# One-hots of source places kept in DRAM by the first edge pass and loaded by the other three, in a four-layer graph network on Trainium2

## The reference, cut to what matters

```python
# L0: two rounds of
agg = segment_sum(x[src], dst, num_segments=n_nodes)
h = (1.0 + eps) * x + agg
h = relu(h @ wa + ba) @ wb + bb
# L3: two rounds of
for r in range(8):
    mask = (edge_type == r)
    s = segment_sum(x[src] * mask[:, None], dst, num_segments=n)
    cnt = segment_sum(mask, dst, num_segments=n)
    out = out + (s / clip(cnt, 1.0)[:, None]) @ W[r]
```

## Time and profile before

| | |
|---|---|
| median of 3 runs | 8339.17 us (8332.13 to 8340.34) |
| profiled execution, first to last instruction | 8339.0 us |
| busy: TensorE matmul, weight load | 77%, 63% |
| busy: VectorE, ScalarE, GpSimd | 59%, 34%, 62% |
| first and second pass | about 1366 to 1760 us and 1805 to 2191 us of the span |
| third and fourth pass | about 7014 to 7592 us and 7650 to 8304 us of the span |
| mean of a group, by starts of its gather: first, second, third, fourth | 2.15, 2.16, 1.60, 1.81 us |

### The profile page before, as it was taken

How to read it: one execution, slowest core, us unless ns; L and a number is a source line. 1 busy time by engine, 2 the same in 40 slices (tenths; PEclk the granted TensorE clock), 3 DMA queues, 4 the chain that set the end, 5 groups by cost and what they waited for, 6 DMA issues and landing times. The chain is left out here.

```text
span 8339.0 us, 233485 instructions
## 1 busy us (share of the span) xinstructions
PE 6397.8 (77%) x55084; PEld 5290.0 (63%) x55143; DVE 4889.1 (59%) x13551; ACT 2862.7 (34%) x8539; POOL 5197.0 (62%) x7407
## 2 busy tenths in 40 slices
PE   2222215767699998999899989999976666888998
PEld 1111113555477776888688868887475556887998
DVE  6333346867556654666466646665432225998998
ACT  3222202545333333333333333333233332222554
POOL 3777755756477776777577757776577774222554
PEclk7555556555599999999999999999555556999999
DMA  5000013434388886888688868887300001332232
GB/s 163 3 3 3 3 38 113 120 96 121 94 223 216 216 204 179 222 222 222 164 222 222 222 163 226 222 222 184 100 6 7 7 7 35 82 82 56 72 73 59
DMA packets 1322718, 1020.15 MB, mean 122 GB/s; under 512 B 479756, under 2 KB 1223586, under 8 KB 1321696
## 3 DMA queue, kind: packets, MB, share of 16 engines
q1 hardware_dynamic: 938010, 667.14, 29.1%
q0 software_dynamic: 134272, 178.98, 11.0%
q10 hardware_dynamic: 250308, 172.51, 7.1%
HBM read 951.88 MB, written 73.77 MB: 123 GB/s over the span
## 5 line engine op out<-in xcount | busy, mean ns | idle before, releaser
L1607 POOL DMA_INDIRECT qg<-q_tab,qidx x2520 | 2388.6, 948 | 928.8 <-issue 692.8
L1762 DVE COPY ps<-b 128x384 f32<-128x384 f32 x1120 | 628.1, 561 | 1355.7 <-ACT h L1727 1348.1
L1156 PE MATMUL ps<-rhs_i,ohi 128*128 128x128 f32 (+2 forms) x8640 | 1215.5, 266 | 210.3 <-issue 198.3
L1156 PEld LDWEIGHTS ps<-rhs_i,ohi 128*128 128x128 f32 (+1 forms) x8640 | 999.1, 162 | 343.2 <-issue 281.9
L1122 POOL COPY near<-x 128x48 bf16 x2160 | 676.0, 351 | 775.9 <-PE ps L1145 433.2
L1676 PE MATMUL ps<-ohm,h 128*128 128x128 f32 x6720 | 1032.1, 290 | 61.3 <-DVE ps L1762 30.7
L1307 POOL DMA_INDIRECT got_m<-y_tab,idx_m x832 | 832.9, 1001 | 344.6 <-issue 246.3
L1720 ACT ACTIVATE h<-ps,b 128x384 f32<-128x384 f32 x1120 | 651.2, 581 | 1049.3 <-PE ps L1658 964.1
L1676 PEld LDWEIGHTS ps<-ohm,h 128*128 128x128 f32 x6720 | 838.5, 191 | 252.0 <-issue 237.0
L406 POOL DMA_INDIRECT list_by_src<-ring,rpos x808 | 783.0, 969 | 333.0 <-issue 254.2
L1781 DVE TENSOR_SCALAR ohm<-iota_row,loc_p,w_p 128x128 f32<-128x128 f32 x3360 | 963.1, 354 | 0.1
(11 more groups left out here) (441 smaller groups left out, 8601.8 us busy)
## 6 DMA issues: line engine op xcount, KB each, us to landing
pb<-p_tab ACTq DMA_DIRECT2D x1680, 96.0 KB
pb<-p_tab SPq DMA_DIRECT2D x1680, 96.0 KB
places<-place_by_turn SPq DMA_DIRECT2D x560, 192.0 KB
places_i<-place_by_meeting SPq DMA_DIRECT2D x360, 256.0 KB, 3.4
places_i<-place_by_meeting SPq DMA_DIRECT2D x720, 128.0 KB, 3.1
qb<-q_tab SPq DMA_DIRECT2D x840, 64.0 KB
qg<-q_tab,qidx POOLq DMA_INDIRECT x2520
nears<-near_by_turn SPq DMA_DIRECT2D x560, 64.0 KB
```

What stands on the lines that cost most here:

```text
L1156: m = pe.matmul(ps[:, bass.ds(to[j], width)], ohi[:, h, j, :], rhs[:, h, j, 0:width], start=False, stop=True, skip_group_check=True)
L1607: pool.indirect_dma_start(qg[:, h, j, :], None, q_tab, IndirectOffsetOnAxis(ap=qidx[:, h, j:j + 1], axis=0)).then_inc(m_got[h], 16)
```

## The change

In the first pass, SyncE writes each group's `oht` to a new table in DRAM, `oht_tab` (180 blocks of 256 KB, 47 MB), after it has been built, and VectorE waits for that write (`i_kept`) before it builds into the same slot again. In the other three passes VectorE builds no `oht`; SyncE loads it from the table into the same ring, once the gather of group n-4 is done (`i_got`). TensorE's gather waits for that load (`i_pl`) instead of for `i_oh`, and its sums wait for `i_oh` too, since `ohi` is still built.

```diff
+        oht_tab = dram("place_onehots", [NIN // 8, P, 8 * P], BF16)
...
+        i_kept = [sem(f"i_kept{h}") for h in range(U)]
...
-                places = sb(f"places_i{turn}", [P, U, M * P], BF16, st)
+                places = sb(f"places_i{turn}", [P, U, M * P], BF16, st) if first else None
...
+                        def keep(k, h):
+                            sp.dma_start(oht_tab[bass.ds(k * U + h, 1), :, :].rearrange("a p e -> (a p) e"), oht[:, h, :]).then_inc(i_kept[h], 16)
+
                         def fetch(k, h):
                             n = k * U + h
+                            if first:
+                                if here(k, h, U):
+                                    sp.wait_ge(i_oh, g0 + n - U + 1)
+                                    keep(k - 1, h)
+                                sp.dma_start(places[:, h, :], place_i[0:1, bass.ds(n * M * P, M * P)].to_broadcast([P, M * P])).then_inc(i_pl[h], 16)
+                                return
                             if here(k, h, U):
-                                sp.wait_ge(i_oh, g0 + n - U + 1)
-                            sp.dma_start(places[:, h, :], place_i[0:1, bass.ds(n * M * P, M * P)].to_broadcast([P, M * P])).then_inc(i_pl[h], 16)
+                                sp.wait_ge(i_got, g0 + n - U + 1)
+                            rows = (oht_tab[bass.ds(k * (U // 2) + h // 2, 1), :, (h % 2) * M * P:(h % 2 + 1) * M * P] if masked else
+                                    oht_tab[bass.ds(n, 1), :, :])
+                            sp.dma_start(oht[:, h, :], rows.rearrange("a p e -> (a p) e")).then_inc(i_pl[h], 16)
                         turns(sp, fetch, rounds)
+                        if first:
+                            for h in range(U):
+                                sp.wait_ge(i_oh, g0 + ng - U + h + 1)
+                                keep(rounds - 1, h)
+                            for h in range(U):
+                                sp.wait_ge(i_kept[h], 16 * rounds)
...
-                            pe.wait_ge(i_oh, g0 + n + 1)
+                            if first:
+                                pe.wait_ge(i_oh, g0 + n + 1)
+                            else:
+                                pe.wait_ge(i_pl[h], 16 * (k0 + k + 1))
...
                             pe.wait_ge(i_rhs, g0 + n + 1)
+                            if not first:
+                                pe.wait_ge(i_oh, g0 + n + 1)
...
-                            dve.wait_ge(i_pl[h], 16 * (k0 + k + 1))
-                            dve.tensor_scalar(oht[:, h, :], places[:, h, :], iota_p[:, 0:1], None, ALU.is_equal)
+                            if first:
+                                if here(k, h, U):
+                                    dve.wait_ge(i_kept[h], 16 * k)
+                                dve.wait_ge(i_pl[h], 16 * (k0 + k + 1))
+                                dve.tensor_scalar(oht[:, h, :], places[:, h, :], iota_p[:, 0:1], None, ALU.is_equal)
```

More of the change, by code:

```diff
@@ L1065, in edge_pass @@
             masked = mode in ("third", "fourth")
-            fourth, third = mode == "fourth", mode == "third"
+            fourth, third, first = mode == "fourth", mode == "third", mode == "first"
             M = 4 if masked else 8
```

## The result

| | before | after |
|---|---|---|
| median | 8339.76 us (8332.13 to 8341.28, 4 runs) | 8407.93 us (8406.37 to 8409.80, 4 runs) |
| span of the profiled execution | 8339.0 us | 8406.7 us |
| ratio after to before | | 1.0083 [1.0068, 1.0097] |

The kernel got slower by 68 us, where +27 was forecast. The direction was right, the size too small, and the measured time lies 13 us above the range, which ended at 8395.

A forecast was written before the change was run, and what follows sets the result against it. TensorE's sequencer was taken to bound the second and most of the first pass, VectorE the fourth, both engines nearly even in the third. On 8339.0 us, 23 + 18 - 11 - 3 + 0 = +27 gave 8366 us; range 8290 to 8395.

The forecast's parts named there:

- Second pass: TensorE's sequencer sets the pace; 180 added waits and 45 register instructions cost +23 us, bounds 0 and +26.
- I take 0.105 us per group for the wait: Sums' added wait on TensorE's sequencer: 0.105 us per group, from 0.32 us for three such instructions; its own duration is 51 ns.
- Third pass: VectorE and TensorE close to even; +0.05 us for each of 360 groups, +18 us, bounds -20 and +38.
- I take half of that: Third pass: half of the +38 us that would come if all four intervals of a round grew by 0.105 us.
- the 1.40 chain: Third pass: gather, mask, gather in 1.40 us; does not run over the sums, so has room for most of the wait.
- Fourth pass: VectorE sets the pace before; afterwards 1.78 us per group against 1.81, so -11 us, bounds -40 and 0.
- The list (1.70, 1.70, 1.78, 1.94): Fourth pass: forecast us from gather to gather by position in the round, longer after and into its top; mean 1.78.
- Starts of the passes: First gather of passes two to four no longer waits for VectorE's builds: about 1 us each, -3 us.
- The writes of the first pass ... 0 us: First pass: SyncE's 180 added writes of 256 KB cost 0 us, bounds 0 and +38.
- The upper bound of +38: First pass: 222 GB/s as ceiling makes a group 2.36 us instead of 2.15; 180 x 0.21 = +38 us.
- third rival: First pass becomes bound by its transfers, VectorE waiting on `i_kept` or places: +38 us, 8404 us; chance 0.10.
- first rival: VectorE's relief wins if the added wait costs nothing where it stands: some -56 us, 8283 us; chance 0.14.

The follow-up runs named there:

- e2: Kernel before plus only the sums' second wait, on `i_oh`, on TensorE in passes two to four; 10523.42 us on another chip, ratio 1.0037 to before.
- e3: Kernel after, but VectorE waits for the table's load before building `ohi`, TensorE's waits as before the change; 10474.01 us on another chip, ratio 0.9989 to before.
- g1: Kernel after with GpSimd making one block copy per group in the fourth pass instead of two, ScalarE three; 10552.09 us on another chip, ratio 1.0058 to before.
- f1: Kernel before plus a second 256 KB load of the places per first-pass group, from DRAM into a spare tile; 8347.69 us, one execution.
- f2: Kernel before plus a 256 KB transfer of places per first-pass group, from DRAM to the table in DRAM; 8344.31 us, one execution.
- e1: Kernel before plus only the first pass's writes, nothing loaded from the table; 10515.08 us on another chip, ratio 1.0026 to before.
- b7: e3 with each first-pass write issued once its group's gather is done (`i_got`), not once its one-hots are built; 8291.35 us, one execution.
- b8: Kernel after with only the first pass's writes issued after the gather instead of after the build; 8378.07 us, ratio 1.0046 to before.

## Why the prediction was right or wrong

**Second pass: right, +23 forecast, +21 measured.** The step "I take 0.105 us per group for the wait" held: 0.104 to 0.109 in e2. The profiled 51 ns would have given half of that. Moving the wait to VectorE (e3) gave the pass its 390 us back.

**Third pass: right within 3 us, +18 forecast, +21 measured**, one step of it by luck. In e3, without the wait, the pass gains 18, where I had put 20. From e3 to the kernel after it grows by 39 us, 0.107 per group: the wait and the round's register cost their full price there. "I take half of that" came near only because the gain and the full price, -18 and +39, add up to about half of the price; the reason that I gave, room in the 1.40 chain, is not what the runs show: against before, the interval of 1.40 grew by 0.08 us and the other three by 0.01, 0.04 and 0.11. VectorE is busy 83%, as foretold.

**Fourth pass: right sign, mis-sized, -11 forecast, -2 measured.** The list (1.70, 1.70, 1.78, 1.94) stands against 1.71, 1.79, 1.78 and 1.94 measured. The term that failed is one of the two 1.70. Where 1.71 was measured, it is 0.80 from gather to sums, my 0.71 and most of the wait, plus 0.90. Where 1.79 was measured, it is 0.73 plus 1.06 (8105.30, 8106.03, 8107.09 above): the gather waits for the mask, and the chain gather, mask, gather, which I had at 1.70 from the earlier trace rows, takes 1.79, since this mask starts 0.98 us after the start of its gather where the next one starts after 0.90. It is 1.77 in this position in e3 as well, without the wait. 360/4 x 0.09 = 8 us, nearly all of the miss. VectorE's 94% against my 70% cost nothing: L1244 had become slow beside GpSimd's copies, as L1212 had been before, and g1 shows that the pass is as long without that.

**Starts of the passes: -3 forecast, -6 measured for all time outside of the passes.** The gap ahead of the second pass became 0.9 us shorter and the one ahead of the fourth 2.1. What lies ahead of the third can't be read so finely: the layers before it take 4820.4 us before and 4826.8 in f1, with the same program there. In the kernel after, no instruction is shown waiting for a load of the table within a pass.

**First pass: wrong, 0 forecast, +33 measured.** The step that failed is "The writes of the first pass ... 0 us". I asked of the added transfers when they would land, whether the bandwidth was there, and whether VectorE had slack, and the answers were right: it waited for none of them. I never asked what they do to the engine that sets the pace. The pass was bound by TensorE's sequencer, and the longest step of that sequencer is a read of SBUF; I had its 593 ns in the earlier trace rows and took them as fixed. The upper bound of +38 came from the third rival. That rival had the right pass and nearly the right size, and the wrong mechanism: by it VectorE would wait for `i_kept` or for places, which it does not, and f1 and f2 at 242 GB/s would be slow, which they are not.

What the first pass's growth rests on is shown up to here: writes out of SBUF issued on `i_oh` lengthen TensorE's register load (e1), the same number of bytes by loads or from DRAM to DRAM does not (f1, f2), and the same writes issued one wait later hardly do (b7, b8), because TensorE's loads then rarely start 0.4 to 1.2 us after an issue, while those of GpSimd that do are lengthened in their turn. That the two meet at SBUF is inferred from this; no run shows the port or the path that they share.

The range ended at 8395 because half of the third rival was left out; the forecast and that rival together, 8404 us, would have been within 4 us of the result, and that by luck, since the rival's mechanism is not what happened. The sentence that the range takes in the forecast with its bounds is wrong too: the bounds of the five terms add up to 8276 and 8438 us. And the first rival's terms (0, -20, -36, -3) give -59 and 8280 us, not -56 and 8283.

## What to carry to other kernels

Where an engine's sequencer bounds a stage, an instruction that a change gives it can cost twice what the profile shows for it (here 0.1 us); look for an engine with slack whose own signal can carry the wait along. A transfer that is hidden by its landing time can still lengthen small register loads out of SBUF on the pacing engine: look at their minimum, median and maximum, and before giving the transfer up, try another event to issue it on, so that the reads fall beside the loads of an engine with slack. Relief of a full engine pays only down to the next limit, so work that one out first.

## What the runs showed of the hardware that was not expected

- TensorE's load of eight registers from SBUF takes 592 ns in the median when undisturbed, and 779 ns in the mean (832 in the median, up to 1153) beside transfers of 256 KB out of SBUF; ScalarE's load of four takes 0.402 us in place of 0.310. GpSimd's, of four too, takes 0.582 in place of 0.321 where it starts 0.55 to 1.2 us after a write's issue (b8). The Trainium skill (SBUF — State Buffer, Who interferes with whom) says that a DMA never contends with a compute engine. If that is meant to cover the register loads of an engine's sequencer too, the first pass would have kept its 390 us, and it took 423: for these loads, with transfers that read SBUF, the measurement decides against it. With transfers that only write SBUF (f1) the trace agrees, 592 ns.
- The table's 256 KB landed 2.6 us after issue, the same 256 KB broadcast from one row of places 3.4 us, and 128 KB 2.1 against 3.1.
- An instruction for a wait that is already met costs TensorE's sequencer 0.104 to 0.109 us in the second pass (e2), of which the profile shows 51 ns.
